# A fused attention, mixing and expert kernel: its last stretch in a new hand-written order, with four plans of slot tiles instead of five

## Time and profile before

| | |
|---|---|
| median of 3 runs | 235.19 us (235.11 to 235.83) |
| profiled execution, its time | 235.37 us |
| profiled execution, its span | 233.6 us |
| busy: PE, DVE, ACT, POOL | 210.1, 147.3, 143.7, 132.0 us |
| mean granted clock of TensorE | 0.97 |

### The profile page before, as it was taken

One profiled execution on the slowest core, in us unless ns is written; L12 is line 12 of the kernel. 1 busy time (PEld: TensorE's weight loads), 2 busy tenths in 40 slices (PEclk: granted clock), 3 DMA queues, 4 the chain that ended last, 5 costly groups with the idle time before them and its releaser, 6 DMA issues.

```text
span 233.6 us, 6687 instructions
## 1 busy us (share of the span) xinstructions
PE 210.1 (90%) x2074; PEld 178.1 (76%) x2074; DVE 147.3 (63%) x489; ACT 143.7 (62%) x473; POOL 132.0 (56%) x336
## 2 busy tenths in 40 slices
PE   6689999999999999999999766997598999999990
PEld 6667877877876786877778453997498899999990
DVE  1687788789797798796989886757412222223313
ACT  2458878878888898888874975545234244444410
POOL 2692795855766787687687367766712233333302
PEclk9799999999999999999999998899979999999996
DMA  6799840050230470000000316433688567782053
GB/s 192 272 355 291 312 148 34 3 180 3 57 128 26 135 240 13 4 25 1 0 26 6 101 31 198 116 127 61 226 297 271 186 220 225 229 231 94 13 175 98
DMA packets 17473, 31.23 MB, mean 134 GB/s; under 512 B 2318, under 2 KB 9617, under 8 KB 17440
## 3 DMA queue, kind: packets, MB, share of 16 engines
q1 hardware_dynamic: 15824, 28.15, 37.6%
q0 software_dynamic: 1184, 2.13, 2.7%
q10 hardware_dynamic: 432, 0.54, 0.7%
HBM read 22.08 MB, written 9.05 MB: 133 GB/s over the span
## 4 chain that ended last, share of the span: by engine, by line
PE 51%; POOL 17%; issue 10%; DVE 10%; ACT 5%; DMA 4%; POOLq 1%; SPq 0%; ACTq 0%; DVEq 0%
PE bank L1141 16%; PE bank L1153 7%; PE bank L947 4%; PE bank L937 4%; POOL table L608 4%; PE bank L902 4%; PE bank L977 3%; PE bank L904 3%; DVE neg_max L1279 2%; POOL qbd_sb L529 2%; POOL o_half L543 2%; DMA table<-rows_tok,slot_at 2%; DMA vec_sb<-vectors 2%; POOL scale_rows L553 2%; ACT p_sb L738 2%
## 5 line engine op out<-in xcount | busy, mean ns | idle before, releaser
L738 ACT ACTIVATE p_sb<-bank,neg_max 128x257 f32<-128x257 f32 x128 | 59.0, 472 | 20.9 <-DVE neg_max L1279 20.1
L1279 DVE TENSOR_REDUCE neg_max<-bank 128x1 f32<-128x257 f32 x128 | 48.3, 424 | 10.0 <-PE bank L1016 4.9
L1141 PE MATMUL bank<-slot_ft,w_now 128*128 128x128 f32 x368 | 50.7, 287 | 2.2 <-ACT slot_ft L820 2.2
L1141 PEld LDWEIGHTS bank<-slot_ft,w_now 128*128 128x128 f32 x368 | 47.6, 203 | 3.9 <-ACT slot_ft L820 2.8
L1537 DVE TENSOR_TENSOR hid_ft<-silu_sb,bank 128x512 f32<-128x512 f32 x23 | 15.8, 688 | 44.0 <-PE bank L1141 44.0
L679 POOL DMA_INDIRECT planes<-y_sb,slot_sb x21 | 20.6, 980 | 38.6 <-ACT y_sb L829 38.0
L747 ACT ACTIVATE pt_sb<-bank 128x512 f32<-128x512 f32 x64 | 35.0, 612 | 0.3 <-PE bank L947 0.3
L947 PE MATMUL bank<-ident,p_sb 128*128 128x128 f32 x256 | 33.3, 273 | 2.0 <-ACT pt_sb L747 2.0
L947 PEld LDWEIGHTS bank<-ident,p_sb 128*128 128x128 f32 x256 | 28.8, 141 | 2.6 <-ACT p_sb L738 2.3
L937 PE MATMUL bank<-kv_sb,qbd_sb 32*128 32x257 f32 x256 | 27.6, 425 | 1.3 <-DVE kv_sb L1291 0.7
L829 ACT ACTIVATE y_sb<-bank,zero_rows,slot_sb 128x128 f32<-128x128 f32 x23 | 10.5, 457 | 26.5 <-PE bank L1153 26.5
(11 more groups left out here) (183 smaller groups left out, 341.1 us busy)
## 6 DMA issues: line engine op xcount, KB each, us to landing
w_now<-w SPq DMA_DIRECT2D x23, 512.0 KB, 3.9
table<-empty_rows SPq DMA_DIRECT2D x3, 1310.0 KB, 9.3
ctx_sb<-ctx_keys SPq DMA_DIRECT2D x7, 512.0 KB, 5.2
wo_sb<-wo SPq DMA_DIRECT2D x8, 256.0 KB, 4.2
slot_sb<-table SPq DMA_DIRECT2D x23, 65.5 KB, 2.9
planes<-zero_rows SPq DMA_DIRECT2D x2, 512.0 KB, 7.0
pt_sb<-planes SPq DMA_DIRECT2D x2, 512.0 KB, 4.7
table<-empty_rows SPq DMA_DIRECT2D x1, 982.5 KB, 10.3
```

The costliest lines, as they stand in the source:

```text
L738: act.activation(p_sb[b % 2][:, g, :], s_bank[g][:, 0:SKV], ACT.Exp, bias=neg_max[b % 2][:, g:g + 1], accum_out=sum_last[:, 0, b, g:g + 1] ...
L1141: last = pe.matmul(bank[2 * m + s % 2][:, tile(c)], w01_now[s % W_BUFS][:, m, tile(c)], slot_ft[s % 2][:], start=True, stop=True)
L1279: dve.tensor_reduce(neg_max[b % 2][:, g:g + 1], s_bank[g][:, 0:SKV], AX.X, ALU.max, negate=True).then_inc(max_ready, 1)
```

## The change

1. **The mix has three products instead of four.** `u_ft` loses the columns of each sequence's first token (they stay zero), the product with `mix_next` reads `u_ft` shifted by one column, and the last tokens come in through `last_diag` and `norm_tok`. The edge terms of the gate are made apart: POOL multiplies `norm_tok` with `edge_w` (one instruction instead of three copies in `edges`), and ACT sums it in the new `gate_edges`, at the head of `take_mix`, into the bias of the tanh.
2. **Four plans:** none behind token tile 5, and tile 6's plan hands out four slot tiles. `full` has two buffers.
3. **SP:** all `value_load`s of a plan's first two tiles come first (`name`), then the wait for the rows, then the slot loads, then the weights; for the others slots before weights.
4. **The end:** PE leaves the loop after batch 29, ACT and DVE after batch 30, and a written list follows. Slot tiles 0 to 6 use bank 0 for the gate half and bank 2 for the up half (`SINGLE = 7`), so that tile 6's late steps have bank 3 and tile 7's bank 7; bank 6 serves tile 5's logits and ranks. Slot tile 0 is turned within batch 30's work. `spread_scales` of tile 7 and the sum of the chosen pairs of tiles 5 to 7 move from POOL to DVE (`choose`). `plan(0, 2)` moves from batch 30 to batch 29, `plan(1, 1)` behind batch 31's last maximum and `take_output(29)`.

```diff
-STAGES = ((3, 1), (4, 2), (5, 2), (6, 2), (NT - 1, SLOT_TILES - 7))
-LATE_TURNS = (3, 5, 7)
+STAGES = ((3, 1), (4, 2), (6, 4), (NT - 1, SLOT_TILES - 7))
+LATE_TURNS = (7,)
+SINGLE = 7
...
-                for s in range(first, heavy):
-                    load_weights(s)
+                ahead = min(end, first + 2)
+                for s in range(first, ahead):
+                    name(s)
                 for i in range(stored, last_tile + 1):
                     sp.wait_ge(rows_stored[i], 16 * TOPK)
                 stored = last_tile + 1
-                load_slots(first)
-                for s in range(first + 1, end):
+                for s in range(first, ahead):
                     load_slots(s)
-                    if s + 1 < end:
-                        load_weights(s + 1)
+                for s in range(first, ahead):
+                    load_weights(s)
+                for s in range(ahead, end):
+                    name(s)
+                    load_slots(s)
+                    load_weights(s)
...
+            def gate_edges(i):
+                act.wait_ge(edges_ready, i + 1)
+                act.activation(edge_sum[i % 2][:], edge_prod[i % 2][:], ACT.Identity, bias=edge_b[:],
+                               accum_out=gate_bias[:, i:i + 1]).then_inc(gate_bias_ready, 1)
             def take_mix(i, src):
+                gate_edges(i)
                 act.wait_ge(mix_done, i + 1)
...
-                pe.matmul(dst[:, C_MIX], u_ft[i % 2][:], mix_u[:], start=True, stop=False)
-                pe.wait_ge(edges_ready, i + 1)
-                pe.matmul(dst[:, C_MIX], first_ft[i % 2][:], mix_first[:], start=False, stop=False)
-                pe.matmul(dst[:, C_MIX], last_ft[i % 2][:], mix_last[:], start=False, stop=False)
-                pe.matmul(dst[:, C_MIX], next_ft[i % 2][:], mix_next[:], start=False, stop=True).then_inc(mix_done, 1)
+                pe.matmul(dst[:, C_MIX], u_ft[i % 2][:, 0:128], mix_u[:], start=True, stop=False)
+                pe.matmul(dst[:, C_V], last_diag[:], norm_tok[:, i, :], start=False, stop=False)
+                pe.matmul(dst[:, C_MIX], u_ft[i % 2][:, 1:128 + 1], mix_next[:], start=False, stop=True).then_inc(mix_done, 1)
```

The new list of PE, from batch 30 on (`scores(B - 1)` is batch 31's):

```diff
+            scores(B - 1)
+            output_product(NT - 2, bank[6])
+            turn_rows(NT - 3, s_bank[3])
+            turn_half(B - 2, 0)
+            turn_slots(0)
+            weigh_values(B - 3)
+            turn_half(B - 2, 1)
+            half_hidden(0, 0)
+            turn_half(B - 1, 0)
+            weigh_values(B - 2)
+            turn_half(B - 1, 1)
+            gate_logits(NT - 3, bank[6])
+            half_hidden(0, 1)
+            weigh_values(B - 1)
+            late_ranks(NT - 3, bank[6])
+            turn_normed(NT - 2, bank[3])
+            turn_slots(1)
+            spread(NT - 1, bank[7])
+            mix(NT - 2, bank[3])
+            output_product(NT - 1, bank[7])
+            half_hidden(1, 0)
+            turn_rows(NT - 2, bank[3])
+            turn_slots(2)
+            gate_logits(NT - 2, bank[3])
+            half_hidden(1, 1)
+            turn_normed(NT - 1, bank[7])
+            mix(NT - 1, bank[7])
+            late_ranks(NT - 2, bank[3])
+            project(0)
+            half_hidden(2, 0)
+            turn_rows(NT - 1, bank[7])
+            half_hidden(2, 1)
+            gate_logits(NT - 1, bank[7])
+            project(1)
+            late_ranks(NT - 1, bank[7])
+            turn_slots(3)
+            for s in range(3, SLOT_TILES):
```

The new list of DVE:

```diff
+            maximum(B - 1, 0)
+            add_output(NT - 2, bank[6])
+            maximum(B - 1, 1)
+            maximum(B - 1, 2)
+            output_statistics(NT - 2)
+            maximum(B - 1, 3)
+            take_output(B - 3)
+            plan(1, 1)
+            scale_tile(NT - 1)
+            spread_scales(NT - 1)
+            take_output(B - 2)
+            top_two(NT - 3, bank[6])
+            choose(NT - 3)
+            take_output(B - 1)
+            take_slots(NT - 3, bank[6])
...
+            plan(1, 2)
+            add_output(NT - 1, bank[7])
+            output_statistics(NT - 1)
+            take_mixed(NT - 2)
+            hidden(0)
+            statistics(1, NT - 2, x2_tok[:, NT - 2, :])
+            top_two(NT - 2, bank[3])
+            choose(NT - 2)
+            hidden(1)
+            take_slots(NT - 2, bank[3])
+            normalise_rows(NT - 2)
+            mixed_statistics(NT - 1)
+            plan(2, 0)
+            top_two(NT - 1, bank[7])
+            choose(NT - 1)
+            normalise_rows(NT - 1)
+            take_slots(NT - 1, bank[7])
+            plan(2, 1)
+            hidden(2)
+            plan(2, 2)
+            plan(3, 0)
+            plan(3, 1)
+            hidden(3)
```

More of the change, by code:

```diff
@@ L177, in build @@
         slot_at = sb("slot_at", [128, NT, TOPK], U32)
-        full = sb("full", [1, E])
+        full = [sb(f"full{n}", [1, E]) for n in range(2)]
         block_base = sb("block_base", [128, E])
@@ L796, in _ @@
             head_normalise(1)
-            for b in range(B):
+            for b in range(B - 1):
                 softmax(b)
@@ L1042, in center_gate @@
                 pe.matmul(dst[:, C_LOGITS], center[:], gate_sb[:], start=True, stop=True).then_inc(gate_c_done, 1)
-            for b in range(B):
+            for b in range(B - 2):
                 if b + 1 < B:
```

422 lines of the change are left out of this document (208 added, 214 removed).

## The result

The change makes the kernel slower: 243.71 us in the median of four runs (241.99 to 247.50), against 235.15 (233.71 to 235.83) of the kernel before on the same chip. The ratio is 1.0348, with a 95% interval of 1.0267 to 1.0430. The forecast was 237.2 and its range ended at 240.6: the direction is right, the size is not. Ratios here leave out the executions that took over 1.5% longer than the fastest of the same kernel; medians and ranges hold all of them. The profiled execution took 244.04 us, its span is 242.2.

The account below looks back on a forecast made before the run. Loop bound by the chain of waits through gate and POOL, not PE; time settled by slot tile 7's start. 178.5 (loop's 0.8 included) against 176.53 gave +2.0 us: 237.4, on the median's scale 237.2, range 233.8 to 240.6.

Parts of the forecast that it names:

- The loop (+0.8): Mix periods: chain through gate and POOL grows 0.26 us in four periods, PE wins 0.22 at tile 0; +0.8 us.
- the 0.48 us of `gate_edges`: ACT ahead of the gate: 0.35 us for 128 columns plus 0.13 for the tanh's wait; bounds 0 to 0.75.
- The sign to look for: In the loop: PE's wait for the normalised tile grows from 0.3 to about 0.8 us a period, period 16.3 us.
- rival B: No change: PE bounds the loop and absorbs the later gate, loop -1.3 instead of +0.8; 235.1 us, chance 0.15.
- Batches 28 to 31: Loop's last batches: weighing batch 28 starts 1.1 us later, second plan ready at 139.9 against 138.2 before.
- rival A: Slower still: PE's clock falls from 142.9 (+1.8), one more DVE instruction is held (0.9); 239.9 us, chance 0.14.
- SP, second plan: Behind the second plan: four value loads take 2.3 us, weights land in 3.8, slot tile 1's gate half at 147.1.
- The third plan and the rows: End: third plan ready at 157.0, tile 6's rows landed by 159, slot tile 3's weights landed at 164.0.
- Low clock (+1.9 behind the idle stretch): Slot tiles from 3 to 7: PE's low clock after eight idle microseconds costs 1.9 us, bounds 0 to 1.9.
- Rival C: Faster: the new end is as dense as meant, PE idles under 6 us before slot tile 3; 233.1 us, chance 0.25.
- The rule weighed: DVE's list from 139 to 157: two-input instructions held repeatedly by POOL; twice 0.4 us would make 238.0.

Follow-up runs that it names:

- e1: Kernel before with the new three-product mix alone, old end and five plans kept: 236.76 us, ratio 1.0110.
- e2: Changed kernel with gate_edges one place earlier on ACT, ahead of the batch's last exponential: 241.60 us, ratio 1.0203.
- e5: Changed kernel with plan(0, 2) put back into batch 30: 245.22 us, ratio 1.0301.
- e13: Kernel of e7 with the plan behind tile 5 put back, five plans in all: 231.72 us, ratio 0.9812.
- e15: e13 with 12 identity products that nobody reads, placed in two waits of PE: 230.13 us, ratio 0.9828.
- e8: e1 with gate_edges ahead of the batch's last exponential, old end kept: 234.65 us, ratio 0.9991.
- e6: Changed kernel with 72 identity products that nobody reads around the turn of slot tile 3: 247.12 us, ratio 1.0504.
- e9: Changed kernel with 48 identity products that nobody reads, in four waits of PE: 241.23 us, ratio 1.0277.
- e3: Changed kernel with SP's old order behind each plan (weights before the rows' wait, slots last): 246.50 us, ratio 1.0404.
- e4: Changed kernel with the third plan ahead of tile 7's best two and tile 6's rows stored early: 242.07 us, ratio 1.0293.
- e12: Changed kernel with the plan behind tile 5 put back, five plans in all: 235.94 us, ratio 1.0040.
- e7: Changed kernel with the edits of e2, e4 and e5, and slot tile 3's weights issued before the wait for rows: 239.07 us, ratio 1.0056.
- e10: e7 with 37 identity products that nobody reads in PE's waits: 235.93 us, ratio 1.0029.

## Why the prediction was right in direction and wrong in size

What failed is the size of the terms on the path, nearly all of them too small. Slot tile 7 came 6.8 us behind the forecast of 178.5, and along the path of the sum that is 1.1 for the loop, 1.0 more up to the second plan, 0.9 for slot tile 1's weights, 0.8 up to the third plan, 0.7 from that plan to the weights' issue, 1.1 for their landing and 1.2 for the four slot tiles behind it, at low clock first. The sum took both weight loads below the median of the earlier trace rows, took the low clock behind the idle stretch at 1.9 us where it cost 2.9, and had `gate_edges` and the new place of `plan(0, 2)` too cheap. What removing a plan does to the idle stretch it did not ask at all.

**The loop (+0.8).** Its mechanism is right and shown by e1 and e2: ACT has no time ahead of the gate, and the chain through the gate sets the period. The term that was mis-sized is the 0.48 us of `gate_edges`. It takes 0.61, and the period grew by 0.4 rather than 0.26. The first period, for which the sum took 0.22 off, grew by as much as the others (0.36). That is +1.8 in all, just inside the bounds that I gave. The sign to look for was wrong: PE's wait for the normalised tile stayed at 0.3 to 0.4 a time, which by my text would have spoken for rival B, while B (a loop bound by PE) was false. DVE's wait for the gate was the row to name.

**Batches 28 to 31.** The edit of `plan(0, 2)` was costed by its delay alone (+1.1 for weighing batch 28). That delay came, as a wait of 1.80 us. What was not asked is what the clock does there: it was at half from 135.4 to 142.3, and the second plan came at 142.85, where the forecast, with the loop's shift, had 140.7. From tile 5's mix it is 14.99 us, forecast 14.0. How much of that is the clock is not shown: in e5, also at half clock, it is 14.25, in e13, at half clock for 3.4 us, 13.38, and in e15, at full clock with five products, 13.21. I had let the clock fall only behind eight idle microseconds, and in rival A at 142.9. e5 shows that this edit alone is not to blame: with 1.06 us of wait, as before, the clock was at half too. So it was in e1 and e8, which have the old end (from 132.9 and from 130.7, each behind a wait of PE for the gate of 0.95 and 0.73 us, where the kernel before had 0.35). What brings it down there stays open.

**SP, second plan.** The four numbers took 2.3 us as predicted (143.03 to 145.39 from first load to first issue). The weights took 4.41 us, not 3.8, still between the ends of the earlier trace rows. That row has a median of 4.0, and nothing in it spoke for less. Its ends are also misread in the range: they allow -0.6 to +1.1 around 3.8 and -0.3 to +1.4 around 3.5, not -0.6 to +1.4 twice. Slot tile 1 started at 150.92: with the loop's shift 3.0 us late, of which 2.1 are the plan's.

**The third plan and the rows.** DVE's list was walked rightly in its order, and the plan came at 161.64, 3.8 us late, mostly by inheritance. But one sentence is wrong by its own rows: with tile 6's second store issued at 156.0 and the 4.10 us of the earlier trace rows its rows land at 160.1, not "by 159". In the changed kernel it left at 160.45 and SP issued the slots at 164.75, so the rows and not the numbers were last. The weights of slot tile 3 took some 4.5 us to land, where I took 3.5 (the gate half stands at 170.38, the issue at 165.79).

**Low clock (+1.9 behind the idle stretch).** From slot tile 3 to slot tile 7 it took 14.87 us; the sum had 13.66. e6 and e9 show 11.9 and 12.0 at full clock, so the cost was 2.9, not 1.9.

**What the sum never priced.** I had the idle stretch in the sum (155.6 to 164.0) and explained it by SP's order and by a plan that stands behind tile 7's ranks. The runs say otherwise: SP's order is worth nothing (e3), the plan's place at most about 2 us (e4), the clock about 2 (e9), the plan that is gone about 7 (e12). Only the last is clear of the noise. These overlap, since the clock also fell in the empty stretch, 2.3 us into it. "None behind tile 5" went into the forecast as fewer value loads and one plan less on DVE. It takes away the only two slot tiles, 5.6 us of PE's work, that can run between tile 7's ranks and the landing of tile 6's rows. Rival C had the same hole: an end "as dense as it was meant" has no work there in any order.

**The rivals.** A was nearest, in size (239.9, still 3.8 short) and in kind, with its place wrong. B and C are out; the decision point of C (under 6 us idle ahead of slot tile 3) was passed by far, 6.46 + 2.99 = 9.45.

**The rule weighed.** One small DVE product was held as at the earlier trace rows: 1.69 us beside POOL's `scale_rows` in the loop:

```profile
127.18 1.69 DVE L1511 TENSOR_TENSOR started_shift<-started,block_shift 1x8 f32<-1x8 f32 x1
```

That agrees with what the Trainium skill states ("SBUF — State Buffer", Who interferes with whom) about two inputs in SBUF. But from 139 to 157 the same kind of instruction took 0.15 to 0.35 us, so the repeated holds that would have made 238.0 did not come. One hold came the other way round, which the sum does not have. The spreading of scales that moved to DVE reads two SBUF inputs for 1.23 us, and POOL's adding of heads beside it took 1.36 us, where it takes 0.32 on its own:

```profile
143.45 1.23 DVE L1423 TENSOR_TENSOR scale_rows<-scales,query_ident 128x1024 f32<-128x1024 f32 x1
143.49 1.36 POOL L558 TENSOR_TENSOR o_half<-o_masked 128x64 f32<-128x64 f32 x1
```

The same pair stands in e2, e7, e12 and e15. Whether it delays anything there was not tested.

## What to carry to other kernels

When a change takes away a stage that hands out work, ask first which wait that work was filling, and price the stage at the length of that wait and the clock behind it. Where several chains meet, keep one piece of work that depends on none of them next to the longest landing. A reduction that moves to another engine belongs in that engine's wait, one place ahead of the instruction that everybody waits for: the same three-product mix made the loop 0.8 us shorter there and 1.8 longer one place later.

## What the runs showed of the hardware

- **The clock falls near short waits, and not always in them.** In the changed kernel it fell at 135.4, 0.8 us into a wait of 1.80 us, with another of 0.96 that had ended at 132.94, and stayed at half until 142.3 though PE was busy for 5.68 of 6.8 us. In e5 it fell at 134.7 while PE was working, behind a wait of 0.96 and ahead of one of 1.06. In e1 and e9 it fell at 132.9 and 132.5, within 0.9 us of the end of a wait of 0.95 and 0.96. In the kernel before, with waits of 0.35, 1.07 and 2.02 us between 130 and 140, it stayed up until 144.6. What decides between them the runs do not show. The Trainium skill ("TensorE: Matmul & The Clock Gate", HAM oscillation) tells of a clock that falls in the waits for loads between two pieces of work. The fall at 162.7 agrees, 2.3 us into the wait for slot tile 3; the one at 135.4 came in a wait for DVE, which that section does not have.
- **The scatter goes with the clock, for the most part.** Executions of e7 span 7.8 us and roughly follow their mean clock (234.46 at 0.976, 242.00 at 0.936). With products in the waits e10's lie within 3.8 us, e9's within 2.6 and e15's within 3.0. Single slow executions at a high clock remain: 238.32 at 0.971 in e8, 238.87 at 0.984 in e10.
- **Products in waits pay only where they fit.** With 12 of them e15's median is 1.6 us below e13's, though the ratios do not differ; 72 around one turn cost e6 more than they gave back, and 24 in the old end gave nothing.
- **A small load behind large ones.** Slot loads of 65.5 KB landed in 1.8 to 2.1 us with nothing just ahead of them, and in 3.5 to 4.0 behind two weight loads of 512 KB on SP's queue; in e7, behind a single one issued 0.6 us earlier, in 4.4.

Not tried: the written order of the four-plan kernel with a slot tile held back for the gap (slot tile 2 worked on behind tile 7's ranks), and whether e13's end is the shortest that this order allows.
